# Writing out the engine loops of a post-norm attention and mixture-of-experts layer as straight code

## The reference, cut to what matters

```
q, k, v = x Wq + bq, x Wk + bk, x Wv + bv        # 16 heads of width 8
a = softmax(q k^T / sqrt(8)) * head_mask
x1 = layernorm(x + (a v) Wo + bo)
shared = gelu(x1 Wfc_s + bfc_s) Wproj_s + bproj_s       # hidden width 512
p = softmax(x1 Wr); the best 2 of 8 experts, their p scaled to sum 1, are the gates
routed = sum over the 2 of gate * (gelu(x1 Wfc[e] + bfc[e]) Wproj[e] + bproj[e])
out = layernorm(x1 + shared + routed)
```

## Time and profile before

| | us |
|---|---|
| median of 3 runs | 655.3 (651.41 to 659.56) |
| the profiled execution | 650.02 |
| its span, first to last instruction | 648.3 |
[...]
| PE busy | 477.3 |
| DVE busy | 401.4 |
| ACT busy | 306.2 |
| POOL busy | 275.4 |
| instructions | 15805 |

### The profile page before, as it was taken

How to read it: one execution, slowest core, us unless ns; L and a number is a source line. 1 busy time by engine, 2 the same in 40 slices (tenths; PEclk the granted TensorE clock), 3 DMA queues, 4 the chain that set the end, 5 groups by cost and what they waited for, 6 DMA issues and landing times. The chain is left out here.

```text
span 648.3 us, 15805 instructions
## 1 busy us (share of the span) xinstructions
PE 477.3 (74%) x5002; PEld 302.3 (47%) x5003; DVE 401.4 (62%) x871; ACT 306.2 (47%) x551; POOL 275.4 (42%) x398
## 2 busy tenths in 40 slices
PE   3898899988998989899961499800299999999000
PEld 2334344444344344434341399800188888888000
DVE  2757775666567576656558577600078888887066
ACT  1147755666556565644534477600054444443025
POOL 5203322323222232321024478877026677678366
PEclk9999975787578586855585599955599999999555
DMA  3222224242233423521205011111671011101093
GB/s 82 61 60 66 75 90 114 85 116 82 61 92 89 115 86 91 133 83 46 73 3 131 26 51 41 42 53 53 159 175 41 32 38 36 34 28 41 8 281 103
DMA packets 72502, 49.84 MB, mean 77 GB/s; under 512 B 9594, under 2 KB 65028, under 8 KB 72468
## 3 DMA queue, kind: packets, MB, share of 16 engines
q1 hardware_dynamic: 67924, 40.92, 23.2%
q0 software_dynamic: 4544, 8.47, 4.0%
HBM read 24.96 MB, written 22.95 MB: 74 GB/s over the span
## 5 line engine op out<-in xcount | busy, mean ns | idle before, releaser
L443 DVE TENSOR_REDUCE row_max<-s_ps 128x2 f32<-128x512 f32 x256 | 165.9, 684 | 98.0 <-PE s_ps L527 94.6
L354 ACT ACTIVATE probs<-st_ps 128x1024 f32<-128x1024 f32 x128 | 129.3, 1024 | 54.2 <-PE st_ps L543 53.4
L527 PE MATMUL s_ps<-k_stack,q_stack 24*128 24x256 f16 x512 | 113.9, 338 | 24.2 <-DVE row_max L443 11.4
L1306 POOL DMA_INDIRECT results<-gated,dest x78 | 89.2, 1144 | 64.1 <-DVE gated L1409 48.1
L1380 ACT ACTIVATE hid_r<-h_ps_r,bias 128x256 f32<-128x256 f32 x156 | 61.1, 474 | 114.7 <-PE h_ps_r L902 114.7
L543 PE MATMUL st_ps<-q_stack,k_stack 26*128 26x256 f16 x512 | 112.4, 339 | 0.4 <-ACT probs L354 0.4
L561 PE MATMUL av_ps<-probs,v_aug 128*32 128x256 f32 x1024 | 97.0, 513 | 0.0
L527 PEld LDWEIGHTS s_ps<-k_stack,q_stack 24*128 24x128 f16 x512 | 37.3, 104 | 101.5 <-DVE row_max L443 50.8
L886 POOL DMA_INDIRECT slots<-rows,slot_at x64 | 70.3, 1099 | 32.1 <-issue 18.9
L914 PE MATMUL y_ps_r<-w,hid_r 128*128 x312 | 59.0, 221 | 0.0
L915 PE MATMUL y_ps_r<-w,hid_r 128*128 x312 | 58.6, 219 | 0.0
(11 more groups left out here) (173 smaller groups left out, 1011.3 us busy)
## 6 DMA issues: line engine op xcount, KB each, us to landing
slots<-empty_row SPq DMA_DIRECT2D x6, 780.0 KB, 6.0
expert<-results SPq DMA_DIRECT2D x16, 256.0 KB, 5.1
w_or_slots<-slots SPq DMA_DIRECT2D x3, 1040.0 KB, 11.0
q_stack<-q_rows SPq DMA_DIRECT2D x64, 48.0 KB
k_stack<-k_rows SPq DMA_DIRECT2D x64, 48.0 KB
w_or_slots<-in_w_fc SPq DMA_DIRECT2D x9, 256.0 KB, 2.8
w_or_slots<-in_w_proj SPq DMA_DIRECT2D x9, 256.0 KB, 2.8
x_t<-in_x_t SPq DMA_DIRECT2D x16, 128.0 KB, 2.2
```

Source lines behind the costliest of these rows:

```text
L354: nc.scalar.activation(probs[:, p % 4], st_ps[:, p % 2], ACT.Exp, scale=SCORE_SCALE).then_inc(exp_done, 1)
L443: nc.vector.tensor_reduce(row_max[:, h], s1_ps[:, h % 2], AX_X, ALU.max, negate=True).then_inc(max_done, 1)
L527: mm = nc.tensor.matmul(s1_ps[:, h % 2, t], band_of(q_stack, b, h, TERM_ROWS)[:, t * P:(t + 1) * P], band_of(k_stack, b, h, TERM_ROWS), st ...
L1306: nc.gpsimd.indirect_dma_start(out=a["results"][:, :], out_offset=bass.IndirectOffsetOnAxis(ap=dest[:, t.buf, half:half + 1], axis=0), in_ ...
```

## The change

`run_steps` and `run_tiles` and the two loops of the routed stage are Python loops now: every step of every engine is built with fixed numbers. Semaphore values and addresses become constants, except the experts' registers, which still come from the table every four steps. `wait_first` becomes a plain wait, and the semaphore `passed` goes. What is computed, the order of instructions on each engine, buffers and DMAs stay.

```diff
-def run_steps(eng, step):
-
-    for t in range(2 * FIRST_LOOP):
-        step(t // 2, t % 2)
-    with eng.Fori(FIRST_LOOP, FIRST_LOOP + LOOPS) as u:
-        step(u, 0)
-        step(u, 1)
-    for t in range(2 * (FIRST_LOOP + LOOPS), BATCHES + 3):
+def run_steps(step):
+
+    for t in range(BATCHES + 3):
         step(t // 2, t % 2)
...
-def wait_first(eng, semaphore, value):
-    eng.wait_ge(semaphore, value)
-    if not isinstance(value, int):
-        eng.sem_inc(PASSED[0], 1)
...
-def run_tiles(eng, step, steps, loop_end):
-
-    for s in range(8):
-        step(s // 4, s % 4)
-    with eng.Fori(2, loop_end) as u:
-        for c in range(4):
-            step(u, c)
-    for s in range(4 * loop_end, steps):
+def run_tiles(step, steps):
+
+    for s in range(steps):
         step(s // 4, s % 4)
...
             pe.wait_ge(loaded, ALL_LOADED)
-            with pe.Fori(EARLY // 4, LOOP_END) as u:
-                four_steps(u)
-            for u in range(LOOP_END, -(-STEPS // 4)):
+            for u in range(EARLY // 4, -(-STEPS // 4)):
                 four_steps(u)
...
             dve.wait_ge(loaded, ALL_LOADED)
-            with dve.Fori(EARLY // 4, LOOP_END) as u:
-                four_steps(u)
-            for u in range(LOOP_END, -(-(SLOT_BLOCKS + GATE_LAG) // 4)):
+            for u in range(EARLY // 4, -(-(SLOT_BLOCKS + GATE_LAG) // 4)):
                 four_steps(u)
```

More of the change, by code:

```diff
@@ L36 @@
 FIRST_LOOP, LOOPS = 2, 5
-PASSED = [None]
 class Batch:
@@ L268, in step @@
                 load_for_moe(sp, a, u, c)
-            run_steps(sp, step)
+            run_steps(step)
         @block.gpsimd
@@ L288, in split_max @@
                 done = (2 * b.n + half) * 3
-                wait_first(pool, max_done, HEADS * b.n + (half + 1) * HALF)
+                pool.wait_ge(max_done, HEADS * b.n + (half + 1) * HALF)
                 if b.since(1):
-                    wait_first(pool, max_turned, 2 * b.n + half - 1)
+                    pool.wait_ge(max_turned, 2 * b.n + half - 1)
                 nc.gpsimd.tensor_scalar(scaled, largest, 1.0 / MAX_UNIT, 1.0, ALU.mult, ALU.mult).then_inc(max_split, 1)
-                wait_first(pool, max_split, done + 1)
+                pool.wait_ge(max_split, done + 1)
                 nc.gpsimd.tensor_scalar(parts[:, 0], scaled, 1.0, 1.0, ALU.mult, ALU.mult).then_inc(max_split, 1)
@@ L420, in _ @@
             act.wait_ge(qk_weights_in, 64)
-            run_steps(act, step)
+            run_steps(step)
         @block.vector
@@ L493, in step @@
                         nc.vector.bn_stats(stats[:, t], z[:, t]).then_inc(stats_done, 1)
-                    wait_first(dve, stats_done, 4 * last.n + 2)
+                    dve.wait_ge(stats_done, 4 * last.n + 2)
                     for t in range(TILES):
@@ L500, in step @@
                     take_turned(nc, dve, a, turned_rows, EARLY_GROUPS - 1)
-            run_steps(dve, step)
+            run_steps(step)
         @block.tensor
@@ L567, in turn_max @@
                 rows = MAX_PARTS * HALF * TILES
-                wait_first(pe, max_split, (2 * b.n + half) * 3 + 3)
+                pe.wait_ge(max_split, (2 * b.n + half) * 3 + 3)
                 nc.tensor.transpose(misc16[0:rows, 0:P], max_parts[:, half].rearrange("p r n -> p (r n)"), ident16[:])\
@@ L657, in _ @@
             pe.wait_ge(qk_weights_in, 64)
-            run_steps(pe, step)
+            run_steps(step)
 I32 = mybir.dt.int32
@@ L769, in load_for_moe @@
     after = FIRST_LOOP + LOOPS
-    if not isinstance(u, int):
+    if FIRST_LOOP <= u < after:
         if c == 0:
@@ L1188, in step @@
                       .then_inc(projected, 1)
-            run_tiles(pe, step, STEPS, TOKEN_TILES // 4)
+            run_tiles(step, STEPS)
         @block.scalar
@@ L1204, in step @@
                     nc.scalar.activation(hid16[:, t.buf, 0], hid[:, t.buf], ACT.Copy, scale=X_UNIT).then_inc(hidden_high, 1)
-            run_tiles(act, step, TOKEN_TILES, TOKEN_TILES // 4)
+            run_tiles(step, TOKEN_TILES)
         @block.vector
@@ L1229, in step @@
                                                    in1=x1_all[:, rows], op0=ALU.mult, op1=ALU.add).then_inc(added, 1)
-            run_tiles(dve, step, STEPS, TOKEN_TILES // 4)
+            run_tiles(step, STEPS)
 def routed_experts(nc, a, w16, b16, pick, ident_h, expert_of, b_units):
@@ L1308, in step @@
                             bounds_check=TOP * TOKENS - 1, oob_is_err=False).then_inc(sent[t.buf], 16)
-            run_tiles(pool, step, SLOT_BLOCKS, LOOP_END)
+            run_tiles(step, SLOT_BLOCKS)
             for buf in range(4):
@@ L1382, in step @@
                     act_.then_inc(activated, 1)
-            run_tiles(act, step, SLOT_BLOCKS + FC_LAG, LOOP_END)
+            run_tiles(step, SLOT_BLOCKS + FC_LAG)
         @block.vector
```

18 lines of the change are left out of this document (8 added, 10 removed).

## The result

The changed kernel takes 616.4 us (median of four, 610.8 to 620.2) where the kernel before takes 657.4 (four, 651.4 to 660.1): ratio 0.936, 95% interval 0.925 to 0.947. It is 6.4% faster, outside the forecast range of 638 to 666. All ratios and intervals here leave out executions in which the chip ran measurably slower than in the others of the same kernel, so they can differ a little from the quotient of the two medians. The two profiled spans are 648.3 and 614.6 us, 33.7 apart.

What follows compares the result with a forecast made beforehand. PE was taken to bound attention at half clock, with waits at full clock, and to pace the routed loop. Shared 0, routed -5.0, steps and code 0, clock 0: -5.0 on 655.3, so 650.3 us, range 638 to 666.

Steps and rivals of the forecast that it cites:

- Part 5: Attention's clock: another pattern but the same share at half clock, 0, plus or minus 9 us.
- Rival (b): Attention: less idle at the turns keeps 2.4 GHz longer; -18 us in all, 637 us; chance 0.16.
- Part 1: Routed stage: PE gains at seven places and POOL can follow; 5.0 us less, range 3 to 7 less.
- Part 2: Shared expert: straight and looped tiles take the same 6.44 us, the branch hidden behind queued matmuls; gain 0.
- Part 3: Attention's ten looped steps: removing branches uncovers a DMA wait at full clock, turns are hidden at half clock; 0.
- Part 4: Attention's code: ten more code blocks may delay SP's issues; taken with the steps at 0, range -2.4 to +6 us.
- the bound of 1.7 us: Attention at full clock: the most one code block was taken to cost, between 0 and 1.7 us.
- rival (a): Full-clock attention steps: code fetches delay SP's chain and the clock is lost; +16 us, 671 us; chance 0.16.
- Rival (c): Routed stage: POOL, stretched by busier DVE and code blocks, ends when it did; no gain, 655 us; chance 0.10.

Runs made afterwards that it cites:

- e9: Changed kernel with 12 unread semaphore increments on PE ahead of the query projection in steps 4 to 13; 714.8 us, ratio 1.005 to the kernel before.
- e12: Changed kernel with two extra copies of the query projection ahead of the real one in steps 4 to 13; 684.0 us, ratio 0.963 to the kernel before.
- e13: Kernel before, all loops kept, with two extra copies of the query projection in the ten looped attention steps; 690.7 us against 710.6, ratio 0.984.
- e3: Kernel before with PE's attention loop alone written out; 636.9 us against 653.8, ratio 0.977.
- e4: Kernel before with the attention loops of SP, POOL, ACT and DVE written out, PE's kept; 647.5 us against 653.8, ratio 0.992.
- after_again: The changed kernel itself, measured once more on another chip; 682.4 us against 710.3 for the kernel before, ratio 0.955.
- e1: Kernel before with only the attention loops written out, on all five engines; 624.4 us against 653.8, ratio 0.956.
- e15: Changed kernel with one extra copy of the query projection in steps 4 to 13; 620.3 us against 656.9 for the kernel before, ratio 0.950.
- e16: Changed kernel with two extra copies of the query projection in all steps 2 to 15; 627.2 us against 656.9 for the kernel before, ratio 0.952.
- e6: Kernel before with POOL's routed-stage loop alone written out; 708.8 us against 710.3, ratio 1.000.

## Why the prediction was wrong

**The clock, Part 5: the step that failed.** "These dips are as deep in the straight step as in the looped", and so "another pattern and the same share, 0 with plus or minus 30 us of low clock". The dip at most turns was not as deep: 1.61 and 1.73 us of idle before, 1.35 after. The 0.33 us of branch was costed only as time, and that the loops also let PE wait longer for ACT (1.37 against 1.03) was not seen. The prediction had its largest term there, 28 us lost to half clock, and asked what the edit does to that term only by looking at one straight step with a DMA wait in it. Measured: 58 us less low clock in steps 5 to 14 and 75 in all of attention, -23.3 us where the sum had 0 and its range 9 either way.

**Rival (b)** was the mechanism: "The clock holds", through less idle at the turns. The reason given against it, that straight steps have the DMA wait in its place, fails in the steps at 79.30 and 94.71, which start without one; where it holds, at steps 8 and 12, the clock did fall. Its price was too small as well: 13 us for a low share of 30%. The share is 41 / 169 = 24% now, and 17 us more went in the steps around the loops. Experiments e9, e12 and e13 show the mechanism from three sides.

**Part 1, routed,** -5.0: right mechanism, size off. The edge of a turn measured as forecast (0.35 us instead of 1.19). But from the first hidden-layer matmul of block 7 to that of block 35 PE took 91.97 us and takes 85.18, 6.8 less for what the sum had as 5.8: seven edges by nearly a full turn each, and a little beside the edges. POOL followed wholly, as its DMAs got shorter (1144 to 1015 ns), not longer: -8.6.

**Part 2, shared,** 0: right. **Part 3, steps at full clock,** 0: right; they did not get shorter, 14.7 to 16.7 us in the eight of the changed kernel. **Part 4, code:** ten more blocks were forecast for the loops; the window of steps 5 to 14 has 12 where it had 2. They are PE's: of q8's blocks of 16 KB the execution has 29 with PE's attention loop alone written out (e3) and 20, as before, with those of the other four engines (e4), which raise q14's 8 KB blocks from 14 to 20. Some issues of SP were long: 1.56 us at 104.86, beside a block that came at 104.99, and this one, beside a block at 116.99 (timeline of SP after):

```profile
116.91 1.46 SPq L241 DMA_DIRECT2D q_rows<-qk_parts  x1
```

PE then waited for the maxima that SP issues behind them, 0.80 us at 111.29 and more at the start of step 8 (timeline of PE after, compare):

```profile
127.99 0.37 PE L513 MATMUL s_ps<-k_stack,q_stack 24*128 24x256 f16 x1 [2.09 <-DMA q_stack<-max_t]
```

The two steps ahead took 16.58 and 16.69 us instead of 15.41, which is inside the bound of 1.7 us for each of the two blocks. But the wait of 2.09 us is longer than any that was forecast, and the clock fell in it (127.6) and stayed low for 27.3 us. So rival (a) came in small: its chain, from SP's late issues to PE's wait to the lost clock, stands in the changed kernel, only at few steps, and the steps in sum got no longer. It is no chance of one execution: after_again and e1 wait 2.07 and 1.94 us at the same step, and in both the clock falls there. That the blocks cause the whole wait was not tried; after_again has no long issue there, only a block at 118.25. In the length of the steps in sum the blocks do not show: the one of 15.41 us from 79.30 has a block too, at 93.03. Beside two of them single issues of SP took 1.46 and 1.56 us, where the one of the earlier trace rows takes 0.33 in the loop. Rival (c) fell with POOL's shorter DMAs.

What remains open: that less idle at the turn made falls rarer is shown. What makes those in the middle of a step, and how the branches and registers of each engine let ACT come late, is not (e3 and e4 say that both sides have a part).

## What to carry to other kernels

Where a kernel runs part of its time at half clock, price an edit of PE's order twice: its own time, and what it adds to or takes from an idle stretch of PE that is there anyway; some 0.3 us a step went with 23 us here. Before writing loops out, try the cheap test of e13: put spare matmuls beside the wait and see if the clock holds. Once the wait at one place is filled, look for the next place, as more filling there gave nothing here (e15 with one copy 620.3 us, e16 with two 627.2). In the changed kernel that place is the wait for the maxima's DMA, behind which 31 of its 41 us of low clock begin.

## What the hardware showed unexpectedly

**Short idle moves the clock.** Stretches of PE's idle that differ by less than a microsecond decide between 41 and 117 us of low clock, where kernels of the same idle lie between 38 and 61. At the one end stand 1.35 us of idle at the turn of a 15.4 us step (the changed kernel), at the other 2.14 (e9).

**The same kernel took 55 us more on some chips.** In groups 2, 3 and 5, each on a chip of its own, every kernel, the one before too, took some 55 us more than in groups 1 and 4, which shared one. In the eleven profiles there PE crawls through tiles 3 to 7 of the shared expert for about 80 us, one or two matmuls between idle stretches marked issue, as long as POOL places rows; then it goes on at its old pace of 1.61 us a tile. From the first shared tile to the first routed transpose that is 138.0 us in after_again and 97.4 in the changed kernel's first profile. The routed stage is longer there too (147.8 against 128.9 us). Timeline of PE, e6, at such a place:

```profile
385.65 0.27 PE L926 MATMUL y_ps<-w,hid 128*128 128x128 f16 x1 [1.13 <-issue]
```

In groups 1 and 4 PE does those tiles at full pace beside the same POOL work. These tiles are straight code in both kernels, so the change has no part in it; what does it was not tried.
